# Second attention layer's gathered rows go straight into the attention's tile, in turns of 128 calls

## The reference

```
h = (x_flat @ W_gat).reshape(M, HEADS, NUM_EXPERTS)
src = jnp.concatenate([edge_index[0], loops])
dst = jnp.concatenate([edge_index[1], loops])
e = jax.nn.leaky_relu(a_src[src] + a_dst[dst], negative_slope=0.2)
e_max = jax.ops.segment_max(e, dst, num_segments=M)
ee = jnp.exp(e - e_max[dst])
denom = jax.ops.segment_sum(ee, dst, num_segments=M)
alpha = ee / (denom[dst] + 1e-16)
msg = h[src] * alpha[:, :, None]
agg = jax.ops.segment_sum(msg, dst, num_segments=M)
```

## Time and profile before

| | us |
|---|---|
| median of 3 runs | 21196.69 |
| lowest, highest | 21191.13, 21208.34 |
| the profiled execution | 21232.24 |
| its span | 21230.7 |
| POOL busy in it | 10288.9 (48%) |
| DVE busy | 7828.5 (37%) |
| PE busy | 7017.9 (33%) |
| ACT busy | 3622.8 (17%) |

### The profile page before, as it was taken

The page is one execution under the profiler, slowest core; times in us unless marked ns, Lnnn a source line. Parts: engine busy times, 40 slices in busy tenths (PEclk is TensorE's granted clock), DMA queues, the critical chain, the costliest instruction groups (busy, mean ns, idle before and its releaser), DMA issues. The chain is left out here.

```text
span 21230.7 us, 223715 instructions
## 1 busy us (share of the span) xinstructions
PE 7017.9 (33%) x79070; PEld 3229.0 (15%) x79070; DVE 7828.5 (37%) x10937; ACT 3622.8 (17%) x6239; POOL 10288.9 (48%) x10259
## 2 busy tenths in 40 slices
PE   0277701000000000089799999860000000000069
PEld 0122301000000000033244444330000000000024
DVE  9866489111111111344477777530111111111244
ACT  0122301000000000034755454540000000000023
POOL 0011288777777777722100000027777777777710
PEclk8588855555555555599888888985555555555589
DMA  0000201111111111154211111331111111111145
GB/s 40 18 30 30 74 21 36 39 39 39 42 43 39 39 39 39 25 130 123 68 39 38 39 38 38 124 121 18 39 39 44 39 39 39 39 42 42 27 96 130
DMA packets 787081, 1073.68 MB, mean 51 GB/s; under 512 B 287476, under 2 KB 503636, under 8 KB 765652
## 3 DMA queue, kind: packets, MB, share of 16 engines
q1 hardware_dynamic: 405844, 612.28, 10.2%
q0 software_dynamic: 343104, 219.83, 6.9%
q10 hardware_dynamic: 37440, 230.74, 3.0%
HBM read 671.93 MB, written 390.08 MB: 50 GB/s over the span
## 5 line engine op out<-in xcount | busy, mean ns | idle before, releaser
L894 POOL DMA_INDIRECT g_got<-table,g_ring x8192 | 8284.3, 1011 | 2497.1 <-issue 2497.1
L1118 PE MATMUL g_rowsP<-g_eye,g_meta 128*20 128x128 f32 x12 | 2.9, 418 | 10768.8 <-DVEq L1162 10768.8
L1010 DVE TENSOR_TENSOR g_z<-g_gs,g_pr 128x512 f32<-128x512 f32 x64 | 44.6, 697 | 8728.9 <-DMA g_gs<-rows 8728.8
L980 ACT ACTIVATE g_out<-g_u 128x512 f32<-128x512 f32 x64 | 40.3, 630 | 10750.5 <-DVE g_d L1025 10750.5
L1118 PEld LDWEIGHTS g_rowsP<-g_eye,g_meta 128*20 128x20 f32 x12 | 1.5, 143 | 10769.4 <-DVEq L1162 10769.0
L2063 POOL DMA_DIRECT2D m_x<-x x64 | 34.3, 537 | 2946.2 <-POOLq L1539 2939.8
L1359 PE MATMUL f_hP<-f_xn,f_w 128*128 128x512 f32 x2048 | 967.5, 595 | 700.3 <-DMA f_xn<-xn 700.3
L1366 PE MATMUL f_oP<-f_hid,f_w 128*128 128x512 f32 x2048 | 962.0, 592 | 0.0
L1388 ACT ACTIVATE f_hid<-f_hP,f_b 128x512 f32<-128x512 f32 x1024 | 648.4, 684 | 1121.5 <-PE f_hP L1359 1121.5
L526 POOL DMA_INDIRECT cb_got<-dst,k_blki x256 | 248.7, 971 | 1138.5 <-DVE cb_le L537 1075.5
L962 POOL DMA_INDIRECT ad<-g_nodes,k_start_row x512 | 695.7, 1359 | 182.2 <-issue 155.4
(11 more groups left out here) (402 smaller groups left out, 15812.1 us busy)
## 6 DMA issues: line engine op xcount, KB each, us to landing
g_got<-table,g_ring POOLq DMA_INDIRECT x8192
f_gate<-gates SPq DMA_DIRECT2D x128, 1024.0 KB
rows<-g_got SPq DMA_DIRECT2D x512, 192.0 KB, 1.9
g_gs<-rows ACTq DMA_DIRECT2D x64, 1536.0 KB, 6.3
state<-g_out ACTq DMA_DIRECT2D x64, 1536.0 KB, 6.0
h_x<-x SPq DMA_DIRECT2D x128, 256.0 KB
xn<-h_xn POOLq DMA_DIRECT2D x128, 256.0 KB
f_xn<-xn SPq DMA_DIRECT2D x128, 256.0 KB, 3.1
```

The costliest lines, as they stand in the source:

```text
L894: pool.indirect_dma_start(self.got[:,par,k,:],None,self.table,bass.IndirectOffsetOnAxis(ap=self.ring[:,par,k:k+1].bitcast(u32),axis=0)).th ...
```

## The change

The new class `DirectGather` is used where `beside` is None, so in layer 1 alone. POOL's calls write straight into `gs`, the half of tile i, and go in turns of 128, one turn for each tile. A turn waits for its indices (the ring now holds 2 x 128 columns) and for `spread` of tile i-2, DVE's last reading of that half. DVE waits for the gathered rows itself (two semaphores, `landed`) instead of for the tile read back. ACT neither waits for stores nor reads `rows`. SP only loads the ring. Layer 0 keeps `Gather`; its object is made later, so its tiles lie elsewhere in SBUF.

```
+class DirectGather:
+    def __init__(self, nc, room, src, table, tile, used):
+        self.nc,self.table,self.src,self.tile,self.used=nc,table,src,tile,used
+        self.ring=room.sb("ring",[P,2,C],i32)
...
+    def sync(self,sp):
+        def load(i,par): sp.dma_start(self.ring[:,par,:],self.src[:,bass.ds(i*C,C)]).then_inc(self.ring_in[par],16)
+        for par in range(2): load(par,par)
+        with sp.Fori(0,COLS//(2*C)-1) as t:
+            for par in range(2):
+                self.landed(sp,t*2+par,par)
+                load(t*2+par+2,par)
+    def landed(self,eng,i,par):
+        for s in self.gathered.sems[par]: eng.wait_ge(s,(i-par)*(4*C)+8*C)
+    def pool(self,pool):
+        with pool.Fori(0,COLS//(2*C)) as t:
+            for par in range(2):
+                i=t*2+par
+                pool.wait_ge(self.ring_in[par],t*16+16)
+                pool.sem_inc(self.gate,1)
+                self.used.before(pool,i,2)
+                pool.sem_inc(self.gate,1)
+                for k in range(C):
+                    pool.indirect_dma_start(self.tile[:,par,k,:],None,self.table,bass.IndirectOffsetOnAxis(ap=self.ring[:,par,k:k+1].bitcast(u32),axis=0)).then_inc(self.gathered.of(k,par),16)
...
-            g=Gather(nc,r,src,table,rows_d)
...
+            direct=beside is None
+            g=DirectGather(nc,r,src,table,gs,spread) if direct else Gather(nc,r,src,table,rows_d)
...
-                    g.tile_stored(act,i)
-                    nc.scalar.dma_start(gs[:,par,:,:],rows_d[:,bass.ds(i*C,C),:]).then_inc(g_in[par],16)
+                    if not direct:
+                        g.tile_stored(act,i)
+                        nc.scalar.dma_start(gs[:,par,:,:],rows_d[:,bass.ds(i*C,C),:]).then_inc(g_in[par],16)
...
-                    landed(dve,g_in,i,par)
+                    if direct: g.landed(dve,i,par)
+                    else: landed(dve,g_in,i,par)
```

More of the change, by code:

```diff
@@ L899, in pool @@
             for par in range(2): self.fetch(pool,t*2+par,par,False)
+class DirectGather:
+    def __init__(self, nc, room, src, table, tile, used):
+        self.nc,self.table,self.src,self.tile,self.used=nc,table,src,tile,used
+        self.ring=room.sb("ring",[P,2,C],i32)
+        self.ring_in=room.pair("ring_in")
+        self.gathered=Rows(room,"gathered",C)
+        self.gate=room.sem("gather_gate")
+    def sync(self,sp):
[17 more added lines that the diff above has]
+                    pool.indirect_dma_start(self.tile[:,par,k,:],None,self.table,bass.IndirectOffsetOnAxis(ap=self.ring[:,par,k:k+1].bitcast(u32),axis=0)).then_inc(self.gathered.of(k,par),16)
 def attention(nc, keep, src, dst, ad, table, rows_d, state_d, bgat, gamma, beta, eye, gates, beside=None, tag="g"):
```

## The result

| | before, us | after, us |
|---|---|---|
| median (20 runs each) | 21211.38 | 21247.86 |
| lowest to highest | 21191.13 to 21247.39 | 21219.8 to 21278.36 |
| span of the profiled execution | 21230.7 | 21251.1 |

The ratio is 1.0018, with a 95% interval of 1.0011 to 1.0025: the change costs some 38 us. That is inside the 0.2% that the prediction called no difference, but the interval leaves out 1, and the sign is the other one: 25 us less was forecast.

The account below looks back on a forecast made before the run. It took POOL's own pace, 1.249 us a call, to bound the gather stage. Gains of 8.1 (tail) and 17 (DVE against POOL) made 25 us, from the median 21196.69 to 21172 us, range 21142 to 21208.

Parts of the forecast that it names:

- The tail: After the gather's last call, `g_z` was to come 2.5 us after its start instead of 10.67; gain 8.1 us, once.
- When DVE works against POOL: Calls lengthened beside DVE's work on a tile: an earlier `g_z` was to make more tiles cheap, gaining 17 us.
- The border: Start of a tile's second next call, 2.50 us after its last call, where `g_z` falls between cheap and expensive.
- cheap: A tile where a call starts ahead of `g_z`, so one fewer is caught: 6.4 us; 20 tiles forecast instead of 5.
- expensive: A tile where `g_z` starts just before the next call, costing POOL 7.5 us; 25 of 30 tiles before.
- Traffic, waits and loads: Removed stores, reads and ring loads, and the new waits on `spread` and the ring, were priced 0 for POOL's path.
- Loop jumps: POOL's jumps back in the gather loop, about 127 before and 15 after, were to gain nothing: 0.
- the rival with the long loop body: The body of 256 calls is fetched again at each of 15 jumps, 4.6 us each: +69 us, 21241; chance 6%.
- Much faster: one more call is caught less.: A later `g_z` spares one call step in each of 31 tiles: 39 us more gained, 21133; chance 11%.
- Turn boundaries and loop jumps ... Nothing is gained: Cutting the gather's 256 turn boundaries to 32 changes nothing, as idle time is 0.3 us before every call: 0.

Follow-up runs that it names:

- experiment 8: The kernel of experiment 4 plus a DVE copy of 512 unread columns between the landing and `g_z`; one run took 21209.64 us.
- experiment 3: The kernel before, staging kept, with turns of 128 calls instead of 16; first to last call 5386.2 us, against 5334.3 before.
- experiment 4: The changed kernel with calls 0 to 63 of a turn on one semaphore, 64 to 127 on the other; 21187.05 us against 21213.08 before, ratio 0.9987.
- experiment 2: The changed kernel with 16 more indirect calls ahead of the gather; first to last call 5373.5 us, against 5375.5 in the changed kernel.
- experiment 6: The changed kernel with four semaphores a half, two alternating for each 64 calls; 21189.69 us against 21215.26 before, ratio 0.9989.
- experiments 1 to 3: The first: changed kernel with already fulfilled waits every 16 calls (ratio 1.0014 to the kernel before) or one at call 64; first to last 5376.9 and 5376.4 us.
- experiment 5: The changed kernel with a turn's first 110, 111, 112 or 120 calls on one semaphore, the rest on the other; first to last 5325.8, 5339.4, 5379.6, 5421.9 us.
- experiment 7: The changed kernel with call k on semaphore k modulo 4 of its half; one run of 21174.39 us beside one of 21224.58 before.

## Why the prediction was wrong

The time lies 40 us above the range's upper end. 15 us of that are in the kernel before, whose median rose from 21196.69 in 3 runs to 21211.38 in 20; the rest is in the sum. By its steps:

- **The tail, -8.1.** Right: 10.67 to 2.53 us, 8.1.
- **When DVE works against POOL, -17.** Right in kind, 5.3 us too large: 11.7. The border was where it was foreseen, and of the 30 tiles with a 5.95 us call 20 are cheap instead of 5, as taken. The saving of 1.1 us a tile is what was too large. It came from two single tiles; over all tiles an expensive one cost 7.4 us before and a cheap one costs 6.5 now, so that 15 x 0.9 = 14 us are saved. The other tiles cost some 0.1 us more than they did, which takes off 2. Part of that are calls beside the operations by which DVE prepares the next tile, some 25 us after `g_z`: the longest of a tile takes 1.09 us now, as a median over the tiles, and took 1.02. The Trainium skill says in SBUF — State Buffer (section "Who interferes with whom") that a probe saw `tensor_tensor` leave DMAs alone, and also that one with both inputs in SBUF contends with GpSimd's reads. The measured 2.55 us call beside the 2.29 us multiplication in experiment 8, as in the earlier trace rows, sides with the second and contradicts the probe for these calls. The 5.95 us call stands beside scans, on which that section says nothing.
- **Traffic, waits and loads, 0.** The price is right: with staging or without, the idle time is the same, 1302.2 and 1301.4 us with turns of 128 (experiment 3 and the changed kernel), 1248.5 and 1248.1 without gaps (the kernel before and experiment 4). The argument for it is not. It took for granted that a call that waits for transfers would show a releaser other than issue; the gaps are waits for landings, and the profile puts them down to issue.
- **Loop jumps, 0, and the rival with the long loop body.** That rival gave +69 and 21241, near the 21247.86 that came, but for the wrong reason. Its 15 jumps lie at a turn's boundary, and there is no gap there; in the kernels without gaps the idle time is 1248 us, jumps included. In the changed kernel nothing is fetched at the jumps, and where it is, in experiment 2, the 3.0 to 3.3 us stay inside POOL's lead. The Trainium skill says in Runtime: NRT & Kernel Launch (section "Instruction fetch mechanics") that a taken branch whose target lies outside the current two-page window waits for its page; experiment 2 agrees for POOL, with these 3 us at each jump.
- **"Much faster: one more call is caught less."** Fell with experiment 8.
- **"Turn boundaries and loop jumps ... Nothing is gained": the step that failed.** The argument was that POOL's idle time is 0.3 us before each of 4096 calls, boundaries included, so a change of the turn's length moves nothing. Idle time "at the tile boundaries or every 256 calls" was named as what would show it wrong, and it came at neither, but 15 calls ahead of each boundary. The row showed that short turns cost nothing; it didn't show that long ones don't. The boundaries did work that no row names: a turn of 16 ends long before 113 calls, and its pair of semaphores has come to rest before it is used again, since the turn waits until the one two before has been stored. The term that was priced 0 is +52.9 us.

Put together: 8.1 + 11.7 gained, 52.9 lost, a loss of 33 us in the stage where a gain of 25 was forecast. Without the gaps the gain is there: 26 us in experiment 4 by its medians. The change with one semaphore for each half of a turn beats the kernel before by 0.13% (0.04 to 0.22), and the one with four semaphores of experiment 6 does by 0.11% (0.01 to 0.2). Neither was run beside the changed kernel on the same chip; that they beat it too follows from its loss to the kernel before.

## What to carry to other kernels

A number that is constant over all calls of a trace is constant only over the lengths of runs that it holds; before a turn, a batch or a loop body is lengthened, ask what each boundary resets. Many indirect calls in a row should signal semaphores that come to rest in turn, as a block of calls for each, rather than few semaphores that are always busy. When idle time grows and the profile puts all of it down to issue, look at the longest single wait and count at which call it stands: the position, and what it doesn't follow, leads to the cause faster than the sum.

## What the runs showed of the hardware

- POOL took 113 of these calls (128 rows of 96 bytes) without any of their semaphores coming to rest, and then its sequencer stopped: in the changed kernel, in experiments 1 to 3 and in experiment 5 with 111, 112 and 120 as gaps of 0.7 to 3.2 us, in experiment 5 with 110 and in experiment 7 hidden by the lead.
- It went on when one of the semaphores that they signal had nothing outstanding: call 113 started 1.78 to 1.82 us after the last landing on it, which is 4.0 to 4.3 us after the start of the last call on it. The landing of a call took a median of 2.4 us from issue.
- POOL's sequencer runs 12 calls, 15 us, ahead. Where the stop ends within this lead nothing of it is to be seen but the later passing of the next wait. The same lead hid the 3.0 to 3.3 us that each jump with a fetch took in experiment 2.
- A call that starts beside DVE's work lasts longer: 2.55 us beside the 2.29 us multiplication and 5.95 us beside the twenty scans, against 0.94.
- What has room for 113 calls isn't known, nor whether it counts calls or their rows: all calls here have 128 rows.
